# One-bank searches and a third weighing bank in the mixed attention of a decoder kernel

## What is computed

```python
q, k, v = _heads(x @ Wq + bq), _heads(x @ Wk + bk), _heads(x @ Wv + bv)   # 16 heads of 16 channels
att = where(causal, einsum('bhqd,bhkd->bhqk', q, k) * scale, -inf)
y = softmax(att) @ v                                                       # 512 x 512, causal: "self"
qc, kc, vc = _heads(x @ Wcq + bcq), _heads(ctx @ Wck + bck), _heads(ctx @ Wcv + bcv)
y = y + softmax(einsum('bhqd,bhkd->bhqk', qc, kc) * scale) @ vc            # 512 x 1601: "cross"
return y @ Wp + bp
```

## Time and profile before

| | before |
|---|---|
| median of 3 runs | 4176.01 us (4174.73 to 4183.14) |
| the profiled execution's own time | 4166.07 us |
| its span | 4164.8 us |
| mixed attention, weighing halves | 221.4 to 1331 us of the span |

### The profile page before, as it was taken

How to read it: one execution, slowest core, us unless ns; L and a number is a source line. 1 busy time by engine, 2 the same in 40 slices (tenths; PEclk the granted TensorE clock), 3 DMA queues, 4 the chain that set the end, 5 groups by cost and what they waited for, 6 DMA issues and landing times. The chain is left out here.

```text
span 4164.8 us, 59026 instructions
## 1 busy us (share of the span) xinstructions
PE 3609.9 (87%) x22188; PEld 2176.9 (52%) x22188; DVE 2279.2 (55%) x4097; ACT 1658.3 (40%) x3027; POOL 968.6 (23%) x1018
## 2 busy tenths in 40 slices
PE   6779999999999785688887678999999996799998
PEld 3533444444443672445445644555555544777877
DVE  6647667566573236444443556677676643534432
ACT  1125546546456221133334224555545564322222
POOL 1100100000000111233323414555545563200000
PEclk9867989979987896789988868999999998899999
DMA  1011211212110320434442043343434411121211
GB/s 66 12 41 44 61 36 42 58 41 52 47 43 18 130 68 23 64 60 65 57 58 65 34 68 56 54 64 58 69 55 64 63 25 71 51 72 60 66 61 61
DMA packets 144627, 229.42 MB, mean 55 GB/s; under 512 B 40916, under 2 KB 90840, under 8 KB 141400
## 3 DMA queue, kind: packets, MB, share of 16 engines
q1 hardware_dynamic: 144344, 225.65, 25.8%
HBM read 99.39 MB, written 8.91 MB: 26 GB/s over the span
## 5 line engine op out<-in xcount | busy, mean ns | idle before, releaser
L918 DVE TENSOR_REDUCE a_mp<-bank 128x1 f32<-128x384 f32 (+2 forms) x1280 | 704.8, 591 | 440.1 <-PE bank L776 426.4
L884 ACT ACTIVATE a_p<-bank 128x512 f32<-128x512 f32 (+1 forms) x1088 | 594.4, 596 | 631.7 <-PE bank L801 602.1
L884 ACT ACTIVATE mx_p<-bank 128x512 f32<-128x512 f32 (+3 forms) x1088 | 548.9, 557 | 503.9 <-PE bank L801 280.9
L918 DVE TENSOR_REDUCE mx_mp<-bank 128x2 f32<-128x768 f32 (+4 forms) x640 | 597.7, 956 | 260.6 <-PE bank L776 167.5
L954 POOL TENSOR_TENSOR a_pair<-a_p 128x512 f32<-128x512 f32 x384 | 489.7, 1307 | 476.9 <-ACT a_p L884 476.8
L776 PE MATMUL bank<-a_ks,a_qs 96*128 96x384 f32 (+2 forms) x1280 | 449.7, 423 | 66.4 <-issue 39.6
L801 PE MATMUL bank<-a_qs,a_ks 98*128 98x512 f32 (+1 forms) x1088 | 421.0, 453 | 42.4 <-DMA a_qs<-a_mt 25.5
L776 PEld LDWEIGHTS bank<-a_ks,a_qs 96*128 96x128 f32 x1280 | 257.3, 203 | 225.6 <-issue 121.3
L801 PE MATMUL bank<-mx_qs,mx_ks 50*128 50x512 f32 (+3 forms) x1088 | 351.6, 505 | 20.7 <-DMA mx_qs<-mx_mt 13.4
L201 POOL TENSOR_TENSOR rs<-ve,neghalf 128x4 f32<-128x4 f32 (+2 forms) x80 | 77.9, 974 | 1244.9 <-DVE ve L196 1201.0
L776 PE MATMUL bank<-mx_ks,mx_qs 48*128 48x384 f32 (+4 forms) x1280 | 322.6, 446 | 4.2 <-DVE mx_mp L918 3.7
(11 more groups left out here) (302 smaller groups left out, 5636.0 us busy)
## 6 DMA issues: line engine op xcount, KB each, us to landing
sf_raw<-in_h_w SPq DMA_DIRECT2D x64, 512.0 KB, 3.5
a_ks<-a_kh SPq DMA_DIRECT2D x96, 192.0 KB, 4.5
ex_w<-in_L_ffn_w SPq DMA_DIRECT2D x16, 1024.0 KB, 5.0
a_qs<-a_qh SPq DMA_DIRECT2D x64, 256.0 KB, 5.9
mx_ks<-mx_kh SPq DMA_DIRECT2D x192, 48.0 KB, 2.1
a_ks<-a_kl SPq DMA_DIRECT2D x48, 192.0 KB, 5.2
mx_qs<-mx_qh SPq DMA_DIRECT2D x128, 64.0 KB, 2.2
mx_rec<-mx_flat SPq DMA_DIRECT2D x128, 64.0 KB, 2.0
```

Source lines behind the costliest of these rows:

```text
L884: act.activation(probs[place % len(probs)][0:kp, q0:T], self.bank(part, n, kb, h)[0:kp, q0:T], ACT.Exp, scale=scale).then_inc(*self.frees( ...
L918: v.tensor_reduce(best[:, tiled * j:tiled * j + tiled, i, ci], bank[:, 0:w] if tiled == 1 else bank[:, :, 0:w], AX.X, ALU.max).then_inc(*s ...
```

## The change

The twins go. In the mixed attention a search takes two single banks from a ring of three (banks 0 to 2), as `a1` and `a2` do with one. Each of its matmuls signals by itself, and each bank is reduced by an instruction of its own. The bank won gives the weighing a ring of three (banks 3 to 5). `a1` and `a2` keep their banks.

```diff
-        self.twins = [Bank(nc, ctx, psum[:, i:i + 2, :], f"{i}{i + 1}") for i in (0, 2)]
...
-        a_banks = Ring(self.banks[0:3] if tiled == 1 else self.twins)
-        b_banks = Ring(self.banks[3:5] if tiled == 1 else self.banks[4:6])
+        a_banks, b_banks = Ring(self.banks[0:3]), Ring(self.banks[3:5] if summed else self.banks[3:6])
...
-                bank = self.take(a_banks, part, n, *at)
-                banks = [bank] if tiled == 1 else [bank[:, r, :] for r in range(tiled)]
-                pe.wait_ge(*self.empty(part, n, *at))
+                for r in range(tiled):
+                    self.take(a_banks, part, n, *at, r)
+                    pe.wait_ge(*self.empty(part, n, *at, r))
                 for r, r0 in enumerate(base):
-                    m = pe.matmul(banks[r][:, 0:w], qs[r0:r0 + 3 * D, j, P * i:P * i + P], ks[r0:r0 + 3 * D, j, 0:w],
+                    m = pe.matmul(self.bank(part, n, *at, r)[:, 0:w], qs[r0:r0 + 3 * D, j, P * i:P * i + P], ks[r0:r0 + 3 * D, j, 0:w],
                                   start=True, stop=job.mask != "causal")
+                    if job.mask != "causal":
+                        m.then_inc(*self.fills(part, n, *at, r))
                 if job.mask == "causal":
                     for r in range(tiled):
-                        m = pe.matmul(banks[r][:, P * i:P * i + P], self.identb[:, :], neg_a[:, :], start=False, stop=True)
-                m.then_inc(*self.fills(part, n, *at))
+                        pe.matmul(self.bank(part, n, *at, r)[:, P * i:P * i + P], self.identb[:, :], neg_a[:, :], start=False,
+                                  stop=True).then_inc(*self.fills(part, n, *at, r))
...
-                bank = self.bank(part, n, *at)
-                v.wait_ge(*self.full(part, n, *at))
-                v.tensor_reduce(best[:, tiled * j:tiled * j + tiled, i, ci], bank[:, 0:w] if tiled == 1 else bank[:, :, 0:w],
-                                AX.X, ALU.max).then_inc(*self.frees(part, n, *at))
+                for r in range(tiled):
+                    v.wait_ge(*self.full(part, n, *at, r))
+                    v.tensor_reduce(best[:, tiled * j + r, i, ci:ci + 1], self.bank(part, n, *at, r)[:, 0:w], AX.X, ALU.max
+                                    ).then_inc(*self.frees(part, n, *at, r))
```

More of the change, by code:

```diff
@@ L169, in fence @@
         nc = self.nc
-        flags = [*(f for name, f in self.flags.items() if name not in running), *(b.freed for b in self.banks + self.twins)]
+        flags = [*(f for name, f in self.flags.items() if name not in running), *(b.freed for b in self.banks)]
         for eng in (nc.tensor, nc.scalar, nc.vector, nc.gpsimd, nc.sync):
@@ L915, in dve_part @@
                 w = P * (i + 1) if job.mask == "causal" else job.cuts[ci][1]
-                bank = self.bank(part, n, *at)
-                v.wait_ge(*self.full(part, n, *at))
-                v.tensor_reduce(best[:, tiled * j:tiled * j + tiled, i, ci], bank[:, 0:w] if tiled == 1 else bank[:, :, 0:w],
-                                AX.X, ALU.max).then_inc(*self.frees(part, n, *at))
+                for r in range(tiled):
+                    v.wait_ge(*self.full(part, n, *at, r))
+                    v.tensor_reduce(best[:, tiled * j + r, i, ci:ci + 1], self.bank(part, n, *at, r)[:, 0:w], AX.X, ALU.max
+                                    ).then_inc(*self.frees(part, n, *at, r))
             elif part == "tops":
-                v.wait_ge(*self.freed("peak", n, cuts - 1, HT - 1, TB - 1))
+                v.wait_ge(*self.freed("peak", n, cuts - 1, HT - 1, TB - 1, tiled - 1))
                 if cuts > 1:
```

## The result

The changed kernel took 4257.46 us (median of four runs, 4241.38 to 4272.19) against 4175.37 of the kernel before on the same chip. The ratio is 1.0193 with an interval of 1.0161 to 1.0224, so it is slower by 82 us. The forecast was 4165 us with a range of 4140 to 4191. The profiled execution has a span of 4240.2 us against 4164.8.

The account below looks back on a forecast made before the run. TensorE, 87% busy, looked like the bound, with weighing waits on ScalarE hiding lost side-by-side matmuls. Stretch terms summed to -10 us, forecast as -11: 4155 us against the profiled 4166.07, so 4165 for the median, range 4140 to 4191.

Parts of the forecast that it names:

- The likeliest case: Whole kernel: -9 to -30 us with -11 the value, at 38%; it alone holds 4146 to 4167 us.
- the search's wait decides: Mixed attention: two-pair halves cost 0.69 us wherever the clock is full, 101 us with others; +20, 4196 us; chance 17%.
- The rival of more half clock: Four stretches: waits in TensorE's gaps bring ten microseconds more at 1.2 GHz in each; +20, 4186 us; chance 10%.
- the netting in the sum: Mixed attention by stretches: weighing waits won against search waits added, -3 -7 -3 -5 +2 +5 +1 = -10 us.
- the 0.69 taken: Search, a half with two pairs: costs TensorE 0.16 + 0.53 = 0.69 us more; one pair costs nothing.
- the 101: Search: 0.69 us in full-clock two-pair halves gives 94 us; with 28 more at 0.24 it makes 101 us.
- The prediction's own sign of being wrong: Search's waits far from 100 us, or the mean clock of the self stretches moving by more than 0.05.
- The dense stretch: Halves following as one, one, two pairs: four pairs in 4.40 us, VectorE's 4 x 1.10, against 4.47 before.
- The weighing's gain: Third weighing bank: nearly all 128.4 us of waits on ScalarE gone, under 30 left; TensorE could win 80 to 110.
- Extra waits and signals at nothing: TensorE's extra waits and signals cost nothing; by the skill's 26.3 ns, 640 signals would be an estimated 17 us.
- the start 0.05 after the release: Search: a pair starts 0.05 us after VectorE frees its bank, so 0.98 us after the pair before.
- VectorE's +94 us: VectorE in the mixed attention: single reductions add 0.147 us a pair, 640 x 0.147 = 94 us, hidden while it has slack.

Follow-up runs that it names:

- The four kernels: Kernel before 4175.37 us; changed kernel with four single search banks, two weighing 4181.94; with three search, two weighing 4333.73; changed kernel 4257.46.
- a wait for each head: Each search matmul waits only for its own bank: 4194.33 us on the changed kernel, 4298.54 us with three search and two weighing banks.
- the experiment with four banks: Changed kernel with four single banks for the search and two for the weighing: 4181.94 us, 1.0021 of the kernel before.
- The filler: Three search, two weighing banks, plus an unread TensorE matmul before each closely following pair: 4329.07 us against 4333.73 without.

## Why the prediction was wrong

**The likeliest case** was -9 to -30 us, and it came out at +82, on the slow side and beyond the slow rival's 4196 us. That rival, the search's wait decides, named the right mechanism and was given 17%. The rival of more half clock had 10%. Both came true together.

**The step that failed** is the netting in the sum. It let one late second weighing pay for one late pair, stretch by stretch, at the clock that each stretch had before. With 80 to 110 us taken as the gain and -10 as the sum, the search's lookahead stood in it at 70 to 100 us. The four kernels price it at 152, with the extra reductions, waits and signals at +7 and the weighing's third bank at -76. The two kinds of waits were not alike: the old ones left the array 9 us idle, the new ones 92.

**What was right in the step.** I sorted the late pairs of the changed kernel's trace by their halves. Of the 88 us that the search's matmuls keep the array idle in the stage, 28 stand before the second pair of a half (84 of 163 are late) and 59 before the first pair of the half after it (137 of 163). After a half with one pair or none 6 of 306 are late, for 1 us in all. So a half with one pair does cost nothing, and one with two cost 0.53 us of idle array, less than the 0.69 taken. The spacing was off the other way: a late pair stands 1.15 us after the one before in place of 0.98. Of that 0.10 is the start after the release, which is the extra wait instruction, and 0.07 is VectorE's later start.

**The clock** is what the step left out. Going from four search banks to three, with two for the weighing, took the stage from 0.82 to 0.76, and the idle time from 68 to 124 us. The 56 us of idle time are below the 101, and the estimate puts 73 of the 152 on the clock. The prediction read the granted clock as 1.00 in cross jobs. It was so in five of the sixteen. The first cross jobs were at 0.85 to 0.90, and two of the four third ones at 0.93 and 0.89 (47.4 and 48.6 us, not 45.4). The prediction's own sign of being wrong was 0.05 in the self stretches. The two that it showed moved by 0.04 and 0.03 (0.59 to 0.55, 0.80 to 0.83), and one of the others by 0.08 upwards (0.75 to 0.83). The clock was lost mostly in the cross jobs, so that sign was put in the wrong place.

**By stretches**, over all batches and in one execution of each kernel. The lost clock is length x (1 - granted clock), in us.

| jobs | before us | changed us | growth | forecast | lost clock grew by |
|---|---|---|---|---|---|
| first self stretch | 119.7 | 131.0 | +11.3 | +5 | +9 |
| three later self stretches | 213.3 | 223.7 | +10.4 | +2 | -3 |
| four first cross jobs | 194.4 | 223.4 | +29.0 | -1.5 | +24 |
| four second cross jobs | 180.5 | 203.9 | +23.4 | -1.5 | +20 |
| four third cross jobs | 180.4 | 188.9 | +8.5 | -7 | +5 |
| three fourth cross jobs | 192.5 | 191.2 | -1.3 | -3 | -12 |
| the last job | 45.8 | 41.6 | -4.2 | -5 | -2 |

The first and second cross jobs hold 52 of the 77 us, and the lost clock of the stage grew by some 42, by the estimate 27 us of these. Where the clock stays at 1.00 the forecast is nearer, and the gain of 1.7 us still did not come. The third cross job of the last batch takes 38.9 us against 39.0, with TensorE's busy time down from 38.15 to 34.15 and its idle time up by as much. Halves without a search have fallen to 1.11 us, and the last job gained about what was forecast.

**The dense stretch** was to give four pairs in 4.40 us, VectorE's pace of 1.10 a pair. VectorE needs only 1.02, the late pairs above stand 1.07 and 1.15 apart, and four pairs take 4.64, more than the 4.47 of before. TensorE's wait and start set the pace there, not VectorE.

**The weighing's gain** was right in kind and nearly in size. Its waits were to fall below 30 us and are 3.6. 80 to 110 us were taken, and 76 were measured in the one order and 104 with a wait for each head (4298.54 - 4194.33). Part of each comes with the clock: by the estimate above, some 34 and 37 us would be left at an unchanged one.

**Extra waits and signals at nothing**, and **the start 0.05 after the release**: the signals and reductions are as good as free (the experiment with four banks, +7 us). The waits are not. The second wait instruction costs 23 us in the changed kernel, and waiting jointly instead of for each head 63, these 23 included. That the first head of a pair could start a whole reduction earlier was never weighed in the prediction.

The Trainium skill's 26.3 ns for each further increment ("TensorE: Matmul & The Clock Gate", "The cost: per-tile semaphore tail") gave an estimated 17 us. The kernel with four banks has all the signals at +7, with 0 to +17 as its interval, so the runs neither need such a tail nor exclude it. The Trainium skill ("TensorE: Matmul & The Clock Gate", "A second HAM failure mode: psum-queue depth-cycling") also ties small idles between groups of matmuls to a clock that swings between its two levels. The filler's 0.77 to 0.81 agrees.

**VectorE's +94 us** is a term of the wrong size. Its busy time in the stage rose by 749.5 - 696.4 = 53 us. The durations of 551 and 619 ns were right, but two in a row take 1.02 and 1.16 us, not 1.10 and 1.24. The reductions of 384 give 424.4 - 389.4 = 35 of the 53. As the experiment with four banks shows, it matters little.

**Left open.** Two pairs of banks for the search together with three for the weighing have no time here. Six banks do not hold them, and a kernel that kept the twins and shared bank 7 with the work beside as the weighing's third bank deadlocks. How much of a lowered clock is the gaps' effect and how much the longer stretch's own can't be told apart here, so the split of 35 and 47 us stays an estimate. Where the last 19 us with a wait for each head go isn't shown either.

## What to carry to other kernels

Count a ring's lookahead in what one user takes: three banks for pairs is one and a half pairs, and the half is lost if both matmuls wait jointly. Put each matmul's wait right in front of it. Read the idle rows of the array and those of the weight loads apart, since a load may wait under a running matmul. A wait that holds the array may lower the clock too, of a stretch that ran at full clock. And do not take the stage's idle time as the most that a bank can win: the third weighing bank won 76 us while idle time rose, because what it removed stood in the busy time.

## What the runs showed of the hardware

- Behind two waits, the last of them late, a matmul started 0.14 or 0.15 us after the reduction's end, in all 227 places of the changed kernel's stage. The second wait is an instruction of its own of 51 ns. Behind a single late wait the matmul started after 0.05 to 0.06.
- Two reductions in a row on VectorE, of 551 ns each, took 1.02 us. The second had started, at 1342.14, before the first had ended, at 1342.23.
- Over four batches the second cross jobs went from a lost clock of 3 us to 24, and TensorE's idle time in them from 6 us to 25. Between single jobs it varies: the third cross job of the third batch went from 0.89 to 1.00. Of the two levels, 1.2 and 2.4 GHz, a granted clock of 0.93 and 0.87 means that the lower one had 14 and 26% of a stretch.
- A stage can have a lower clock with no more idle array: 0.76 with 71 us idle (three search banks, two weighing, a wait for each head) against 0.85 with 66 us before.
- Between equal kernels the time follows the granted clock, an estimated 0.65 us for each microsecond of lost clock. In the changed kernel VectorE's reductions of 384 took 552 ns on average while TensorE was at the lower level and 551 at the upper, and ScalarE's exponentials of 512 took 595 at both.
